# Typed rows of 26 node blocks during the in-degree count, out-degrees counted in the typed layer, marks strewn among the fetches

## The reference

```python
edge_index = jnp.stack([src, dst])
x = _layernorm(x + _L0_gnn_ref(x, W_e, b_e, W_n, b_n, src, dst, edge_type_3, node_type_3))
x = _layernorm(x + _L1_gnn_ref(x, weight, bias, edge_index, edge_weight))
x = _layernorm(x + _L2_gnn_ref(edge_index, x))
x = _layernorm(x + _L3_gnn_ref(x, edge_attr_64, src, dst, 6250, weight, weight_edge, bias))
```

```python
parts = [relu(x)] + [segment_sum(where(edge_type == t, relu(x[src] @ W_e[t].T + b_e[t]), 0), dst) for t in range(3)]
updated = select(node_type, concatenate(parts) @ W_n[type].T + b_n[type])
```

## Time and profile before

| | us |
|---|---|
| median of three runs | 5259.34 |
| the profiled execution, its own time | 5261.47 |
| its span from first to last instruction | 5259.7 |
| TensorE busy | 3770.5 |
| VectorE busy | 3260.5 |
| GpSimd busy | 2254.5 |
| ScalarE busy | 1204.4 |

### The profile page before, as it was taken

One profiled execution on the slowest core, in us unless ns is written; L12 is line 12 of the kernel. 1 busy time (PEld: TensorE's weight loads), 2 busy tenths in 40 slices (PEclk: granted clock), 3 DMA queues, 4 the chain that ended last, 5 costly groups with the idle time before them and its releaser, 6 DMA issues. The chain is left out here.

```text
span 5259.7 us, 100150 instructions
## 1 busy us (share of the span) xinstructions
PE 3770.5 (72%) x38930; PEld 2751.6 (52%) x38930; DVE 3260.5 (62%) x4529; ACT 1204.4 (23%) x2110; POOL 2254.5 (43%) x2050
## 2 busy tenths in 40 slices
PE   4357755555555555377777676389999599989997
PEld 3345555555555555366666666345555244444444
DVE  7796898999999999455555554756666600230012
ACT  0025655555555555100000000400000200010000
POOL 0051378777777777577777777000000003000300
PEclk9998898999999999688998988699999799989998
DMA  9646797999999999865666656198888267656654
GB/s 315 212 115 238 236 343 276 327 346 340 336 338 340 343 344 330 222 165 166 171 165 165 169 162 158 22 332 305 301 305 304 91 203 227 198 165 202 217 187 142
DMA packets 695303, 1252.28 MB, mean 238 GB/s; under 512 B 366488, under 2 KB 511532, under 8 KB 685772
## 3 DMA queue, kind: packets, MB, share of 16 engines
q1 hardware_dynamic: 564028, 779.03, 46.1%
q10 hardware_dynamic: 60300, 314.88, 15.4%
q0 software_dynamic: 70576, 152.66, 11.4%
HBM read 792.49 MB, written 506.62 MB: 247 GB/s over the span
## 5 line engine op out<-in xcount | busy, mean ns | idle before, releaser
L1398 POOL DMA_INDIRECT big<-typed_msgs,big x988 | 1198.1, 1213 | 376.9 <-issue 307.8
L1446 PE MATMUL psum<-big 128*128 128x98 bf16 x7936 | 859.4, 208 | 649.8 <-DVE big L1428 629.4
L1446 PEld LDWEIGHTS psum<-big 128*128 128x128 bf16 x7936 | 766.0, 97 | 694.1 <-DVE big L1428 673.6
L2088 PE MATMUL psum<-big 128*128 128x512 bf16 (+1 forms) x4704 | 992.1, 373 | 82.6 <-DMA big<-adj 82.6
L1673 PE MATMUL psum<-big 128*128 128x192 f32 x3648 | 743.1, 364 | 307.8 <-DMA big<-typed_msgs,big 302.9
L1581 POOL DMA_INDIRECT big<-typed_msgs,big x836 | 830.8, 994 | 275.3 <-issue 244.8
L1673 PEld LDWEIGHTS psum<-big 128*128 128x128 f32 x3648 | 686.9, 215 | 371.8 <-issue 248.5
L1447 PE MATMUL psum<-big 128*128 128x49 bf16 x7936 | 845.5, 190 | 0.9 <-issue 0.9
L1448 PE MATMUL psum<-big 128*128 128x49 bf16 x7936 | 842.4, 186 | 2.7 <-issue 2.7
L1448 PEld LDWEIGHTS psum<-big 128*128 128x128 bf16 x7936 | 791.7, 100 | 3.1 <-issue 3.1
L2088 PEld LDWEIGHTS psum<-big 128*128 128x128 bf16 x4704 | 460.4, 98 | 605.9 <-DMA big<-adj 83.0
(11 more groups left out here) (320 smaller groups left out, 2732.9 us busy)
## 6 DMA issues: line engine op xcount, KB each, us to landing
wadj<-big ACTq DMA_DIRECT2D x248, 784.0 KB
big<-wadj SPq DMA_DIRECT2D x124, 1568.0 KB, 7.3
big<-adj SPq DMA_DIRECT2D x210, 896.0 KB, 4.8
adj<-big ACTq DMA_DIRECT2D x62, 1568.0 KB
big<-staged SPq DMA_DIRECT2D x247, 384.0 KB, 3.3
staged<-big SPq DMA_DIRECT2D x61, 1536.0 KB
big<-edge_feats SPq DMA_DIRECT2D x456, 128.0 KB, 3.0
edge_feats<-in_edge_attr SPq DMA_DIRECT2D x1, 51562.5 KB, 163.3
```

Source lines behind the costliest of these rows:

```text
L1398: pool.indirect_dma_start(out=sgot4[:, c, u, 0:D], out_offset=None, in_=typed_rows, in_offset=bass.IndirectOffsetOnAxis(ap=pairs4i[:, g, u ...
L1446: pe.matmul(to[:, 0:2 * NB], lo, hi_b[:, q, t, 0:2, 0:NB], start=True, stop=False)
L2088: last = pe.matmul(ps[c % 2][:, 0:len(blocks) * P], terms_[:, k, b * D:(b + 1) * D], ring_a[:, m % RA, 0:len(blocks), s * P:(s + 1) * P], ...
```

## The change

Three things move.

1. *Typed rows of 26 blocks in the in-degree count* (`EARLY = 26`). The helpers for a block's typed rows are moved ahead, and the count's loop on TensorE is written out: after batch n it does as many steps of the typed rows as `(n + 1) * 28 // 101` says. ScalarE gets the copies, SyncE the stores, behind all that its stream has there. The slot stage makes the other 23 blocks, in its first steps.
2. *Out-degrees in the typed layer.* The 101 batches leave the slot stage. In the typed layer VectorE makes one pair of one-hots every four groups and TensorE sums it two groups later. The keys of the out-degree count are kept at the end of the big SBUF tensor, and the groups use five PSUM tiles instead of six.
3. *Marks among the fetches.* GpSimd issues the first four fetches at once, and from the fifth on three marks before each fetch. The mark load moves from step 12 to step 36, the forward fill from step 20 to step 42, the pair store from step 23 to step 45.

```diff
+        kept_at = big_words - CW
+        kept_keys = big[:, kept_at:big_words].bitcast(BF16)
+        sbkt, sloc = kept_keys[:, 0:CW], kept_keys[:, CW:2 * CW]
...
+        EARLY = 26
+        def rows_out(act, b):
+            act.wait_ge(s_z, b + 1)
+            at_least(act, s_mst[b % MZ], 16 * (b // MZ))
+            act.copy(zrows[b % MZ][:, 0:T * D], ps[4][:, 0:T * D]).then_inc(s_ze, 1)
...
+        def typed_out(pe, b):
+            pe.wait_ge(s_me, b + 1)
+            at_least(pe, s_ze, 2 * b)
+            for t, to in enumerate((ps[4], ps[6], ps[7])):
...
                 sp.dma_start(edge_pairs[FRONT + MARKS:EROWS, :].rearrange("(p c) r -> p (c r)", p=TAILP), tail_pairs).then_inc(s_pads, 16)
+                for b in range(EARLY):
+                    sp.wait_ge(s_ze, 2 * b + 2)
+                    sp.dma_start(typed_msgs[b * P:(b + 1) * P, :], zrows[b % MZ]).then_inc(s_mst[b % MZ], 16)
...
                 act.wait_ge(s_x, 32)
+                for j in range(EARLY + 2):
+                    if j < EARLY:
+                        turned(act, j, 0)
+                    if 1 <= j < EARLY + 1:
+                        relus(act, j - 1, 0)
+                    if j >= 2:
+                        rows_out(act, j - 2)
...
-                in_steps(pe, PAIRS, ins)
-                ins(PAIRS, DST_REST)
+                pe.wait_ge(s_x, 32)
+                done = 0
+                for n in range(HB):
+                    hist_sum(pe, in_count, n, n % 2, opens=n == 0, closes=n == HB - 1)
+                    while done < (n + 1) * (EARLY + 2) // HB:
+                        if done < EARLY:
+                            turn_x(pe, done, 0)
+                        if 1 <= done < EARLY + 1:
+                            messages(pe, done - 1, 0)
+                        if done >= 2:
+                            typed_out(pe, done - 2)
+                        done += 1
...
+                pe.wait_ge(s_ze, 2 * EARLY)
...
-        MARK_LOAD, MARK_SCAN = 12, 20
-        AHEAD = 44
+        MARK_LOAD, MARK_SCAN = 36, 42
...
-                    if 3 <= n < NB + 3:
-                        b = n - 3
+                    b = EARLY + n - 3
+                    if EARLY <= b < NB:
                         sp.wait_ge(s_ze, 2 * b + 2)
...
-                for b in range(NB):
+                def mark(b):
...
+                for b in range(GR):
+                    fetch(b)
                 pool.wait_ge(s_same, 1)
...
+                marked_to = 0
+                for b in range(GR, NB):
+                    for m in range(marked_to, min(NB, marked_to + 3)):
+                        mark(m)
+                        marked_to = m + 1
+                    fetch(b)
...
-                outs(0, AHEAD)
                 dve.wait_ge(s_chunk, 16 * 4)
...
-                        outs(*shares[n])
...
+        OUT_EVERY = NG // HB
+        PQ = 5
...
+                def out_hot(g):
+                    j, r = divmod(g, OUT_EVERY)
+                    if r == 1 and j < HB:
+                        hist_hot(dve, sloc, sbkt, HB + j, j * TT, (HB + j) % 2, out_lo, out_hi)
...
+                        out_hot(g0 + pos)
                         own(i, pos, own_)
...
+                        c, r = divmod(g0 + pos, OUT_EVERY)
+                        if r == 3 and c < HB:
+                            hist_sum(pe, out_count, HB + c, (HB + c) % 2, opens=c == 0, closes=c == HB - 1, lo_hot=out_lo, hi_hot=out_hi)
```

More of the change, by code:

```diff
@@ L241, in build @@
         next_i = next_c.bitcast(I32)
+        kept_at = big_words - CW
+        kept_keys = big[:, kept_at:big_words].bitcast(BF16)
         keys = []
-        for _ in range(4):
+        for _ in range(2):
             c, at = cut(at, CW // 2)
             keys.append(c.bitcast(BF16))
-        dbkt, sbkt, dloc, sloc = keys
+        dbkt, dloc = keys
+        sbkt, sloc = kept_keys[:, 0:CW], kept_keys[:, CW:2 * CW]
+        keys += [sbkt, sloc]
         masks_at = at
@@ L376, in along_t, with turned, relus, turn_x @@
             return v.rearrange("p (g t) -> p g t", t=TU).unsqueeze(2).to_broadcast([P, TG, n, TU])
+        EARLY = 26
+        def turned(act, b, b0):
+            act.wait_ge(s_xT, b + 1)
+            if b >= b0 + 2:
+                act.wait_ge(s_m, b - 1)
+            act.copy(xTs[b % 2], ps[2][:, 0:P]).then_inc(s_xTe, 1)
+        def relus(act, b, b0):
+            act.wait_ge(s_m, b + 1)
+            if b >= b0 + 2:
+                act.wait_ge(s_z, b - 1)
+            for t in range(T):
+                made = act.activation(mTs[b % 2][:, t * P:(t + 1) * P], ps[3][:, t * P:(t + 1) * P], ACT.Relu,
+                                      bias=beT[:, t:t + 1])
+            made.then_inc(s_me, 1)
+        def rows_out(act, b):
+            act.wait_ge(s_z, b + 1)
+            at_least(act, s_mst[b % MZ], 16 * (b // MZ))
+            act.copy(zrows[b % MZ][:, 0:T * D], ps[4][:, 0:T * D]).then_inc(s_ze, 1)
+            act.copy(zrows[b % MZ][:, T * D:KINDS * D].rearrange("p (k c) -> p k c", k=2),
+                     psum[:, 6 * 512:8 * 512].rearrange("p (k c) -> p k c", k=2)[:, :, 0:T * D]).then_inc(s_ze, 1)
+        def turn_x(pe, b, b0):
+            if b > b0:
+                pe.wait_ge(s_xTe, b)
+            pe.transpose(ps[2][:, 0:P], X[:, b * D:(b + 1) * D], ident).then_inc(s_xT, 1)
+        def messages(pe, b, b0):
+            pe.wait_ge(s_xTe, b + 1)
+            if b > b0:
+                pe.wait_ge(s_me, b)
+            for t in range(T):
+                made = pe.matmul(ps[3][:, t * P:(t + 1) * P], weT[:, t * D:(t + 1) * D], xTs[b % 2], start=True, stop=True)
+            made.then_inc(s_m, 1)
+        def typed_out(pe, b):
+            pe.wait_ge(s_me, b + 1)
+            at_least(pe, s_ze, 2 * b)
+            for t, to in enumerate((ps[4], ps[6], ps[7])):
+                made = pe.matmul(to[:, 0:T * D], mTs[b % 2][:, t * P:(t + 1) * P], wnT[:, (t + 1) * T * D:(t + 2) * T * D],
+                                 start=True, stop=True)
+            made.then_inc(s_z, 1)
         in_count = ps[5][:, 0:NB]
@@ L1018, in _, with fetch @@
                         in_=mark_v[:, b:b + 1], in_offset=None, bounds_check=beyond, oob_is_err=False).then_inc(s_marks, 16)
[L1019 to L1026, removed]
+                def fetch(b):
                     n = JB + b
@@ L1145, in store @@
                     act.copy(tabs[:, k, 0:3, :], ps[k][:, 0:3 * SLOTS].rearrange("p (r g) -> p r g", r=3)).then_inc(s_slot_e, 1)
[L1147 to L1165, removed]
                 for n in range(GB + 1):
@@ L1171, in _ @@
                         store(n - 1)
[L1172 to L1177, removed]
+                    b = EARLY + n
+                    if EARLY <= b - 1 < NB:
+                        turned(act, b - 1, EARLY)
+                    if EARLY <= b - 2 < NB:
+                        relus(act, b - 2, EARLY)
+                    if EARLY <= b - 3 < NB:
+                        rows_out(act, b - 3)
             @block.tensor
             def _(pe):
[L1181 to L1203, removed]
                 for n in range(GB):
                     k = n % 2
-                    if n < NB:
-                        turn(n)
+                    b = EARLY + n
+                    if b < NB:
+                        turn_x(pe, b, EARLY)
                     pe.wait_ge(s_sb_st, n + 1)
@@ L1213, in _ @@
                     last.then_inc(s_slot_T, 1)
-                    if 1 <= n < NB + 1:
-                        message(n - 1)
-                    if 2 <= n < NB + 2:
-                        rows(n - 2)
-                    outs(*shares[n])
+                    if EARLY <= b - 1 < NB:
+                        messages(pe, b - 1, EARLY)
+                    if EARLY <= b - 2 < NB:
+                        typed_out(pe, b - 2)
         typed_rows = typed_msgs.rearrange("n (t f) -> (n t) f", t=KINDS)
```

44 lines of the change are left out of this document (25 added, 19 removed).

## The result

The changed kernel takes 5450.9 us (median of 4 runs, 5438.7 to 5455.5) against 5260.0 us in the runs beside it: ratio 1.036, 95% interval 1.0341 to 1.0376. The prediction was 5402 us, range 5350 to 5470. The profiled run took 5452.8 us, its span is 5451.0 us, its mean granted TensorE clock 0.898 (0.934 before).

What follows compares the result with a forecast made beforehand. VectorE paced the in-degree count and GpSimd's gathers the typed layer; the slot stage loop began at 356.8 us. 5261.5 + 155 - 62 + 50 = 5404, with the median 2 us lower: 5402 us, range 5350 to 5470.

Steps and rivals of the forecast that it cites:

- A: In-degree count with 26 blocks' typed rows added: +155 us (+131 to +170), with TensorE waiting for a typed_msgs store.
- the store passes the queue: Rival, in-degree count: the store lands soon after its issue at 177.1, TensorE resumes at 182; A +131, 5378 us; chance 0.08.
- the rule that the prediction quotes there: Trainium skill, for DMA queues: descriptors of one queue are consumed in ring order, yet a later transfer may complete first.
- last sum near 358: Sign in the profile after: the in-degree count's last sum on TensorE ends at 358 us instead of 204.8.
- 79 batches in 22 steps: 22 x 7.0 = 154: In-degree count after the store lands at 204: the remaining batches, with blocks between, at 7.0 us a step, 154 us.
- the block, taken at 2.48 us: In-degree count, one block's typed rows on TensorE: transpose 0.08, message matmuls 0.67, output matmuls 1.72 us.
- B: Slot stage without the out-degree batches and the early blocks' typed rows: 562 us against 624, -62 (-100 to -30).
- The marks' price of 17 us: Slot stage, steps 13 to 33: marks among GpSimd's fetches put step 33 at 453 us, typed rows alone about 436.
- The stalls: Slot stage: 12.0 us at the mark load, about 8 at the forward fill, 18.9 at the pair store; 39 together.
- C: Typed layer with the out-degree count: 101 one-hot pairs each hold up GpSimd's gathers 0.5 us, +50 (+34 to +109).
- gathers held longer: Rival, typed layer: each one-hot pair holds up gathers for over 1 us; C +109, 5461 us; chance 0.10.
- Faster: Rival: block 0's store lands before TensorE needs it, so nothing stands still; A +33, B -85, C +20, 5227 us; chance 0.05.

## Why the prediction was right, and where it was off

- **The number**: 5450.9 us lies in the range of 5350 to 5470, but only because that was widened to take in the neighbours. The forecast's own range ended at 5450, and A, at 192.9 us, lies beyond its own upper bound of 170. The mechanism was right; that a mis-sized A stayed inside the range is in part luck.
- **Where TensorE stands, and what ends it**: right. Forecast from 85 to 204 us and ended by the landing of a typed_msgs store; measured 88.7 to 203.0, and that. The store on another queue and the copy in pieces show the mechanism from two sides: on SyncE's queue the stores wait their turn behind the whole copy, beside it they advance packet for packet. The rival that the store passes the queue (TensorE back at 182) fell. Of the rule that the prediction quotes there, the runs bear out the half that one queue is consumed in ring order.
- **Size of A**: off by 38 us (155 forecast, 192.9 measured), and nearly all of the miss; the sign "last sum near 358" failed (397.75). The term that was mis-sized is the step: "79 batches in 22 steps: 22 x 7.0 = 154" was (397.75 - 203.0) / 22 = 8.85 us a step, 195. Nearly all of these 41 us are the block, taken at 2.48 us and 4.27 on average in the count; the batches of a step took 3.65 and 5.23 us where 3.55 and 5.15 were reckoned, about 2 us in all. The block was wrong in two ways. The larger is the clock: a block in the count takes 2.76 us at 1.00 and up to 5.05 near 0.5, and 22 x (4.27 - 2.76) = 33 us. The run with extra matmuls shows the same from the other side (output matmul from 650 to 538 ns, sum 14.5 us earlier); no run held the clock at 1.00 all through. The smaller is a reading: the 1.72 us of the output matmuls were read from weight load to weight load, but the next batch's matmuls begin later than its first weight load. Matmul to matmul, the same step has 502.98 - 501.04 = 1.94 us:

```profile
501.04 2.10 PE L1199 MATMUL psum<-wnT,big 128*128 128x384 f32 x6
...
502.98 0.95 PE L366 MATMUL psum<-big 128*128 128x49 bf16 x16
```

  With that a block is 2.76 us at full clock, and 22 x 0.28 = 6 us of the miss are this. What lowers the clock stays open. It isn't the pause: the copy in pieces has none, and its blocks are as long. Nor is it idle time between batches alone: the kernel before has more of it, at 1.00.
- **B** (-62 forecast, -55.8 measured): right, and by its steps. The loop waits for the chunk and starts at 517.8 us, which less A is 324.9 (forecast 322); steps of 3.53; rounds of 5.1, with step 33 at 646.0, less A 453 (forecast 453); the last step ends at 760.3, less A 567.4 (forecast 562). The stalls were 47 us instead of 39. The marks' price of 17 us inside that sum is 24.8 and 16.8 in the runs that take them out, and 14.3 and 13.4 in their slot stages alone.
- **C** (+50 forecast, +54.2 measured): right in size and mechanism. 0.52 us per pair against 0.5, and 0.17 with shorter instructions.
- **The rivals**: gathers held longer (5461 us) came nearest to the time, for the wrong reason. Its C of 109 was not there; A's excess stood in for it. *Faster* (5227 us) would have failed without the pause too: the copy in pieces has none, and takes 5341.5 us, since A is then 75 us and not 33.
- What the parts cost is seen by medians: the count moved +9, the marks among the fetches +25, the early blocks +47 (5341.5 with the copy in pieces, against 5294.4), their stores behind the copy +109: together 190.

## What to carry to other kernels

A store whose landing frees a buffer must not be queued behind a bulk copy, and a second queue isn't a way out by itself: there it advances one small packet for each of the copy's large ones (24 us gained here, against 109 with the copy in pieces). Cut the copy and put the pieces between the stores. And a duration taken at full clock holds only where the clock is full: between short bf16 batches, a block of f32 matmuls cost up to 1.8 times as much here (5.05 us against 2.76). How busy TensorE was did not tell it beforehand. Take a duration from one matmul to the next, not from the weight loads, which run ahead. Where VectorE's work must lie beside GpSimd's gathers, short instructions are cheaper than long ones with the same elements.

## What the runs showed of the hardware that was not expected

- Two queues on the same DMA engines alternated 614 to 613 packets at 60 KB against 4.1 KB each, so a store of 0.59 MB took 27.6 us beside the copy.
- 808 matmuls more made the in-degree count 14.5 us shorter, with the granted clock at 0.91 to 0.92 from 120 to 200 us instead of 0.76 to 0.79.
- The count with TensorE busy for 95.6 of 162 us ran at a clock of 1.00; with the f32 blocks in it, busy for 129.4 of 156 us, it ran at 0.77.
- Behind pair stores of 124 rows the share of the DMA engines was 0.25, at 105 GB/s; with the stores cut at row 112 it stayed at 1.00, and the wait behind them fell from 20.2 to 6.6 us. By the Trainium skill (DMA: Bandwidth & Descriptors, "Why a DMA increments its semaphore by 16 and not by 1") the number of engines is the largest up to 16 that divides the slowest dimension on both sides, which would be 4 for 124 rows and 16 for 112; the share of 0.25 agrees.
